# Sums of column passes kept column by column in PSUM, and y read and written across the rows

## The reference, cut to what matters

```python
def step(h, inp):
    ul, dl, bl, cl = inp
    dA = jnp.exp(dl[..., None] * A)
    h = dA * h + (dl * ul)[..., None] * bl[:, :, None, :]
    y = jnp.einsum('bkdn,bkn->bkd', h, cl)
    return (h, y)
...
y = y0 + y1 + y2 + y3 + y4 + y5 + y6 + y7
```

## Time and profile before

| | |
|---|---|
| median of three runs | 15633.26 us (15625.79 to 15644.69) |
| span of the profiled execution | 15638.3 us (the page gives no other time of that execution) |
| mean granted TensorE clock | 0.946 of full |
| instructions | 128313 |

### The profile page before, as it was taken

One profiled execution on the slowest core, in us unless ns is written; L12 is line 12 of the kernel. 1 busy time (PEld: TensorE's weight loads), 2 busy tenths in 40 slices (PEclk: granted clock), 3 DMA queues, 4 the chain that ended last, 5 costly groups with the idle time before them and its releaser, 6 DMA issues.

```text
span 15638.3 us, 128313 instructions
## 1 busy us (share of the span) xinstructions
PE 12948.2 (83%) x42560; PEld 7615.4 (49%) x42560; DVE 14604.3 (93%) x8593; ACT 8897.0 (57%) x8571; POOL 13820.4 (88%) x5892
## 2 busy tenths in 40 slices
PE   7887888878888788887888878888788887888878
PEld 4553355533555335553355533555335553355533
DVE  8998989989899899998999989999899998999988
ACT  4455745457454674556744567445674456744567
POOL 7997979979799798997989978899788997889978
PEclk8999999999999999999999999999999999999999
DMA  5662256622566225662256622566225662256622
GB/s 180 211 214 104 86 180 213 211 101 86 185 212 211 100 84 187 214 210 98 82 193 212 210 95 81 193 213 213 93 78 199 213 211 92 76 200 213 211 87 77
DMA packets 696921, 2473.06 MB, mean 158 GB/s; under 512 B 79292, under 2 KB 101064, under 8 KB 696264
## 3 DMA queue, kind: packets, MB, share of 16 engines
q1 hardware_dynamic: 696264, 2464.85, 45.9%
HBM read 2448.81 MB, written 15.73 MB: 158 GB/s over the span
## 4 chain that ended last, share of the span: by engine, by line
POOL 47%; issue 18%; DVE 13%; PE 11%; DMA 7%; ACT 3%; DVEq 0%; POOLq 0%; SPq 0%; ACTq 0%
POOL room L1043 24%; POOL room L1086 7%; DMA room<-bc_rows 7%; POOL room L1052 5%; POOL room L1078 4%; POOL room L1089 4%; DVE room L1279 4%; DVE room L1212 3%; PE bank L621 3%; POOL room L1033 3%; DVE room L1220 3%; PE bank L556 2%; PE bank L407 2%; DVE u L1169 1%; DVE room L1299 1%
## 5 line engine op out<-in xcount | busy, mean ns | idle before, releaser
L1043 POOL TENSOR_TENSOR room<-room 128x1024 f32<-128x1024 f32 x3072 | 7161.8, 2369 | 0.6
L1212 DVE TENSOR_TENSOR_SCAN room<-bank,room 128x1024 f32<-128x1024 f32 x3072 | 6936.5, 2278 | 75.7 <-POOL room L1043 71.7
L556 PE MATMUL bank<-room,identity 128*128 128x256 f32 x24576 | 5985.2, 389 | 188.5 <-DVE room L1220 188.5
L556 PEld LDWEIGHTS bank<-room,identity 128*128 128x128 f32 x24576 | 4758.9, 195 | 1333.5 <-DVE room L1220 269.6
L825 ACT ACTIVATE bank<-room,a 128x1024 f32<-128x1024 f32 x3072 | 3411.3, 1115 | 3273.9 <-DVE room L1212 3258.4
L621 PE MATMUL bank<-room,identity 128*128 128x512 f32 x6144 | 3011.5, 641 | 860.8 <-DVE room L1299 728.4
L1279 DVE TENSOR_TENSOR_SCAN room<-bank,room 128x1024 f32<-128x1024 f32 x1536 | 3431.5, 2274 | 54.1 <-POOL room L1086 33.6
L1220 DVE TENSOR_TENSOR room<-room,bank 128x1024 f32<-128x1024 f32 x2304 | 2764.1, 1200 | 387.3 <-PE bank L526 374.1
L621 PEld LDWEIGHTS bank<-room,identity 128*128 128x128 f32 x6144 | 1204.8, 204 | 2667.3 <-issue 1257.2
L1086 POOL TENSOR_TENSOR room<-room 128x1024 f32<-128x1024 f32 x768 | 2224.3, 2919 | 56.2 <-ACT room L908 26.7
L1052 POOL TENSOR_TENSOR room<-room 128x1024 f32<-128x1024 f32 x768 | 1817.1, 2366 | 344.1 <-DVE room L1212 343.0
(11 more groups left out here) (115 smaller groups left out, 8767.1 us busy)
## 6 DMA issues: line engine op xcount, KB each, us to landing
room<-bc_rows SPq DMA_DIRECT2D x4608, 512.0 KB, 4.4
wx<-in_w_x SPq DMA_DIRECT2D x65, 162.0 KB
bc_rows<-xdbl SPq DMA_DIRECT2D x72, 128.0 KB, 5.3
pictures<-in_x SPq DMA_DIRECT2D x8, 768.0 KB, 10.9
out_x<-pictures SPq DMA_DIRECT2D x8, 768.0 KB, 7.2
win<-in_w_in SPq DMA_DIRECT2D x16, 288.0 KB, 6.1
room<-in_w_in SPq DMA_DIRECT2D x16, 288.0 KB, 5.0
room<-in_w_out SPq DMA_DIRECT2D x16, 288.0 KB, 5.6
```

The costliest lines, as they stand in the source:

```text
L556: ins = nc.tensor.matmul(dst[line][part], identity[:, :], src[line][part], start=(i == 0 and n == 0 and line == 0), stop=(n == N - 1 and l ...
L1043: nc.gpsimd.tensor_tensor(source0[:, g % SOURCES, :], du0[:, j, :], b_ring0[:, g % BROWS, :], ALU.mult).then_inc(S["source"], note("source ...
L1212: nc.vector.tensor_tensor_scan(run(state0[:, g % STATES, :]), run(whole(DECAY0[g % 2])), run(source0[:, g % SOURCES, :]), 0.0, ALU.mult, A ...
```

## The change

In the passes along columns the sum in YACC is kept in column order, 32 columns of 32 pixels one behind the other, so that `sum_states` writes in runs along the lines. The reordering moves to `y`, which stays row by row: `begin_sums` reads y with a step of 32 words as the moving operand, and `collect` writes it with that step. Counts and sizes of the instructions are the same. The helper's name `columns` in layer 1 is changed, since a new function takes it.

```diff
+def columns(ap):
+
+    return ap.rearrange("p (r c) -> p c r", c=SIDE)
...
                     for h in range(2):
-                        nc.tensor.matmul(bank[:, YACC + h, :], identity[:, :], y[:, j, halves(h)],
-                                         start=True, stop=False)
+                        before = y[:, j, halves(h)]
+                        if SCANS[i][1] == "cols":
+                            before = columns(y[:, j, :])[:, h * (SIDE // 2):(h + 1) * (SIDE // 2), :]
+                        nc.tensor.matmul(bank[:, YACC + h, :], identity[:, :], before, start=True, stop=False)
...
-                src, dst = stored(state0[:, g % STATES, :]), lines(whole(YACC), SCANS[i][1])
+                order = "mirror" if SCANS[i][1] == "mirror" else "rows"
+                src, dst = stored(state0[:, g % STATES, :]), lines(whole(YACC), order)
                 for h in range(2):
                     for line in range(2):
-                        part = lines_in(SCANS[i][1], h, 2, line)
+                        part = lines_in(order, h, 2, line)
...
-                nc.scalar.activation(y[:, j, :], whole(YACC), ACT.Copy).then_inc(S["ysum"], note("ysum", (i, j)))
+                dst, src = y[:, j, :], whole(YACC)
+                if SCANS[i][1] == "cols":
+                    dst, src = columns(dst), src.rearrange("p (c r) -> p c r", c=SIDE)
+                nc.scalar.activation(dst, src, ACT.Copy).then_inc(S["ysum"], note("ysum", (i, j)))
...
-                def columns(j):
+                def steps_by_columns(j):
```

More of the change, by code:

```diff
@@ L922, in scans1 @@
                 softplus1(b, 0, WORK[0])
-                columns(0)
+                steps_by_columns(0)
                 softplus1(b, 1, DECAY_ROWS)
@@ L943, in scans1 @@
                     if n == 2 and j + 1 < J:
-                        columns(j + 1)
+                        steps_by_columns(j + 1)
                     if j == J - 1 and n in (8, 9):
```

## The result

The changed kernel takes 15793.0 us (15786.3 to 15801.1, four runs) against 15638.3 us before (median of four runs; the three of the table above gave 15633.3): a ratio of 1.0102, 95% interval 1.0088 to 1.0116. That is +155 us where I had forecast +193, and 15793 us where I had forecast 15830: inside the range, and slower as forecast.

A forecast was written before the change was run, and what follows sets the result against it. VectorE's work plus its stalls was taken as the bound; collect +0.95 and begin_sums +1.9 us made TensorE 2.85 us late, less idle 24.1 us an image, 193 us over eight: about 15830 us (+1.25%), range 15,640 to 16,250.

The forecast's parts named there:

- What bounds the kernel: Layer 0 passes: VectorE's own work, 48.6 us a pass, plus its stalls, chiefly waiting for TensorE's spread of a C row.
- Part 1, sums in PSUM: Sums of states in column passes write PSUM contiguously instead of with a step of 32 words: 0 gain.
- Part 2, collect: ScalarE's copy of the finished sum writes SBUF with a step of 32 words: +0.95 us, bounds 0 and +0.95.
- Part 3, begin_sums: Four TensorE records read SBUF with a step of 32 words: +1.9 us, bounds 0 and +6.3.
- rival 1: TensorE reads the strided operand twice at the strided pace, +6.3 us in begin_sums: +613 us, 16,250; chance 0.15.
- rival 2: The strided read is free on TensorE: +20 us, 15,655, or 15,635 with a free collect; chance 0.17.
- The chain: Collect, begin_sums, then the spread: lateness beyond TensorE's idle of 0.59 us (1.1 us with j = 1) stalls VectorE in full.
- d: TensorE's lateness at a column pass's start, collect's and begin_sums' added times: 2.85 us.
- The clock term I leave as it is: TensorE's low-clock stretches at pass starts may move, at 1.6 us each; nothing was added for them.
- a changed clock record at the pass starts: Named sign, in the profile of after, that the forecast would be wrong.
- My two lengths for the profile of after: Column passes: 50.5 us with j = 1 instead of 48.7, the others near 53.
- Rival 3: Begin_sums fills TensorE's idle, low clock stays away: -77 us, 15,557; decides only with d below about 2.2 us; chance 0.06.

The follow-up runs named there:

- experiment 3: Kernel before with only the column passes' sums written in contiguous runs of 32 words, y left as it was: 15642.6 us, ratio 1.0000.
- experiment 10: Kernel after with y's column sum in PSUM by pairs of columns, so collect and begin_sums touch runs of two adjacent words: 15630.2 us, ratio 0.9997 against before.
- Both fillers: Kernel before with an overwritten contiguous matmul ahead of begin_sums from the fourth pass on: 256 columns 15563.6 us (0.9954), 384 columns 15521.6 us (0.9929).
- the doubled one: Kernel before with the contiguous begin_sums issued twice in the column passes: 15650.2 us, ratio 1.0006.
- the two doubled kernels: Kernel before with contiguous begin_sums issued twice in column passes, alone (15650.2 us, 1.0006) or with collect's strided write too (15721.8 us, 1.0060).
- the filler ahead of the strided read: Kernel after with an overwritten matmul of 256 columns ahead of begin_sums: 15801.3 us, ratio 1.0108 against the kernel before.
- experiment 9: Both kernels with begin_sums and sums issued later on TensorE in each pass's first units: before 15934.9 us (1.0196), after 15960.0 us (1.0212).
- the runs of the table: One profiled execution each of kernels with the old TensorE order, split into lateness and clock cost in the column passes.

## Why the prediction was right, point by point

- *What bounds the kernel*: right. VectorE's work of 48.6 to 48.9 us a pass stays, and the loss is its wait for the spread, +160.7 us (forecast +190).
- *Part 1, sums in PSUM, 0*: right. 379 ns a record in both orders, and a ratio of 1.0000 when changed alone. The page PSUM — Partial Sum Buffer of the Trainium skill (Specifications), by which this part would have gained, doesn't hold for these fp32 matmuls: neither steps of 32 words (experiment 3) nor of two words (experiment 10) cost anything.
- *Part 2, collect*: +0.89 us, forecast +0.95. A strided write costs ScalarE nearly what a strided read does.
- *Part 3, begin_sums*: +1.70 us, forecast +1.9. The records start 0.86 us apart instead of 0.43. The pace is halved, where ScalarE's loss in ns would have given a little more. The upper end, 6.3 us (rival 1, whose own sum comes to 615 us, not 613), and the lower, nothing (rival 2), are both out at full clock.
- *The chain*: right. With d = 2.59 us the same sum gives 169 us; at full clock passes 14 and 15 are 51.46 and 50.70 us, 1.96 and 1.98 above 49.50 and 48.72, where 2.59 - 0.59 = 2.00 was to be.
- *"The clock term I leave as it is"*: right in its sum and by luck. The term is worth 93 us before and 84 after, but not because nothing moved. The prediction named a changed clock record at the pass starts as a sign that it was wrong, and that sign came: from 30, 0 and 19 starts with j = 0, 1 and 2 to 11, 20 and 13, and from 177 to 280 us of low clock. The sum stayed in good part because 81 of these us fell on the strided begin_sums, where they cost nothing. My two lengths for the profile of after (50.5 us for j = 1, near 53 for the others) came out, in the passes shown, as 52.35 and 51.46 or 50.70. Each half of the change alone shows how large the term can be: the read gives +60 us, the write -59, and both together +155. Had the change been the write alone, the method would have forecast +17 and missed the sign.
- *Rival 3, faster by the clock*: its mechanism exists. Both fillers fill the idle time, the clock falls less often, and the kernel is faster than before. The write alone is faster too, though there the idle time is not filled but moved ahead of begin_sums. In the kernel after the lateness of 2.59 us, above the rival's own bound of 2.2, decides, and the low clock did not become less.

The difference between forecast and result: 24 us from the two sizes (193 to 169), 9 from the clock term, and the rest, some 5 to 8 us, lies outside the column passes and within the scatter of the runs.

**Open.** Two pairs with the same lateness show that the strided read brings more low clock than a dense matmul of the same length: 184 against 55 us, and 280 against 37. The mean granted clock of every run of the four kernels, profiled or not, agrees: 0.946 to 0.948 with the read alone against 0.950 to 0.952 with the doubled one, and 0.943 to 0.945 after against 0.951 to 0.953. Where the pass starts fall shifts with every change of length, and no run here held that fixed; but the two doubled kernels have the clock fall in none of 96 starts, spread over eight images, and the strided ones in 22 and 44, which place alone would hardly give. That the array works at half its rate during the read, and that this is what the clock answers to, is only argued; the filler ahead of the strided read, which adds work, did not bring the clock back (235 us, and 43 starts).

## What to carry to other kernels

Read a matmul's duration in both layouts before moving a stride from one side to the other: here the strided PSUM write was free, and the strided SBUF read and write nearly doubled two instructions on the one chain that stalled VectorE. If an access must jump, let it jump between pairs of adjacent words: 592 ns a record on TensorE and 1.06 us on ScalarE, against about 1.04 us a record and 1.91 us for single words. And where TensorE idles for half a microsecond ahead of thin matmuls that something waits for, see whether the clock falls there; an overwritten matmul of 384 columns, which pushed the work behind it into that gap, made this kernel 0.7% faster, while an order that left the same place empty for 2.7 us came out 2% slower.

## What the runs showed of the hardware that was not expected

- An fp32 matmul whose moving operand steps 32 words an element starts a record every 0.86 us at 2.4 GHz, where a contiguous one needs 0.43; four records fill 3.68 against 1.98 us. At 1.2 GHz the stride costs nothing: in the runs of experiment 9 four records with the clock low throughout fill 3.78 us, strided (33 cases) or contiguous (6 cases).
- ScalarE writes SBUF with that step in 1914 ns and reads with it in 1994 ns, against 1023 and 1040.
- The clock is a term of the size of the change itself: in the runs of the table it is worth 9 to 93 us in the column passes alone, and a longer instruction (collect, 0.89 us) made the kernel 59 us faster, with the clock low for 61 us of the column passes where it was 177. In that kernel TensorE's idle stands ahead of begin_sums and no longer ahead of the 12-row products.
